# A block of attention and experts on one core: the first head group's rows written by their own products, and the first steps put in another order

## The reference

```python
# x: (4, 256, 128), ctx: (4, 64, 64); 16 heads of 8 columns
xn = layernorm(x)
q, k, v = xn @ Wq + bq, xn @ Wk + bk, xn @ Wv + bv            # per head
y  = softmax(causal(q k^T / sqrt(8))) v
qc, kc, vc = xn @ Wcq + bcq, ctx @ Wck + bck, ctx @ Wcv + bcv
y  = y + softmax(qc kc^T / sqrt(8)) vc
x  = x + y @ Wp + bp
h  = layernorm(x)
w  = weights of the 8 best of 32 experts by sigmoid(h @ Wr + br), normalized
x  = x + shared(h) + sum_e w_e * ((silu(h Wg_e + bg_e) * (h Wu_e + bu_e)) Wd_e + bd_e)
```

## Time and profile before

| | |
|---|---|
| median of 3 runs | 198.81 us (198.47 to 198.85) |
| the profiled execution | 198.38 us, its span 196.6 us |
| TensorE busy | 186.8 us (95%), 1254 matmuls |
| VectorE, ScalarE, GpSimd busy | 149.9, 137.6, 111.6 us |
| chain that ended last | PE 73%, POOL 14%, issue 5%, DVE 4% |

### The profile page before, as it was taken

The page is one execution under the profiler, slowest core; times in us unless marked ns, Lnnn a source line. Parts: engine busy times, 40 slices in busy tenths (PEclk is TensorE's granted clock), DMA queues, the critical chain, the costliest instruction groups (busy, mean ns, idle before and its releaser), DMA issues.

```text
span 196.6 us, 4006 instructions
## 1 busy us (share of the span) xinstructions
PE 186.8 (95%) x1254; PEld 138.8 (71%) x1254; DVE 149.9 (76%) x343; ACT 137.6 (70%) x280; POOL 111.6 (57%) x181
## 2 busy tenths in 40 slices
PE   7969999999999999998999999799999999999992
PEld 2537667777778777765775888588788888888671
DVE  2999997677659765896683879759777888887982
ACT  3546899787899887987788584875655556555471
POOL 6889994556396699839936567776622333000020
PEclk9999999999999999999999999999999999999999
DMA  4454423232243333500211103030000000000003
GB/s 114 107 144 122 122 71 79 57 80 68 63 105 95 77 80 76 132 12 17 66 42 43 40 0 80 12 77 17 0 0 0 3 0 0 0 2 0 3 0 107
DMA packets 20434, 10.40 MB, mean 53 GB/s; under 512 B 11881, under 2 KB 18542, under 8 KB 20414
## 3 DMA queue, kind: packets, MB, share of 16 engines
q1 hardware_dynamic: 19290, 9.24, 18.6%
q0 software_dynamic: 672, 0.69, 1.4%
q10 hardware_dynamic: 452, 0.23, 0.5%
HBM read 4.51 MB, written 0.52 MB: 26 GB/s over the span
## 4 chain that ended last, share of the span: by engine, by line
PE 73%; POOL 14%; issue 5%; DVE 4%; DMA 1%; ACT 1%; DVEq 0%; POOLq 0%
PE psum L1752 10%; PE psum L1417 7%; PE psum L1418 7%; PE psum L1419 7%; PE psum L1518 5%; PE psum L1574 5%; PE psum L1611 5%; PE psum L1599 5%; POOL hid_lo L739 4%; PE psum L1621 4%; PE psum L1517 3%; PE psum L1579 3%; POOL ckey_rows L457 3%; PE psum L1747 3%; PE psum L1583 2%
## 5 line engine op out<-in xcount | busy, mean ns | idle before, releaser
L982 ACT ACTIVATE gate<-psum,bias_cols 128x512 f32<-128x512 f32 (+2 forms) x35 | 23.5, 674 | 24.2 <-PE psum L1419 24.2
L844 ACT ACTIVATE probs<-psum 128x512 f32<-128x512 f32 x64 | 36.2, 596 | 2.3 <-PE psum L1579 1.1
L739 POOL TENSOR_TENSOR hid_lo<-hid,hid_hi 128x512 fp32r<-128x512 f32 x13 | 16.8, 1289 | 30.2 <-ACT hid_hi L991 30.1
L1361 DVE SCALAR_TENSOR_TENSOR gated<-psum,bias_cols,gate 128x512 f32<-128x512 f32 x32 | 24.0, 749 | 10.7 <-ACT gate L982 10.6
L1518 PE MATMUL psum<-key_blocks,query_rows 96*128 96x512 f32 x48 | 24.1, 544 | 0.0
L1373 DVE TENSOR_TENSOR hid<-gated,psum 128x512 f32<-128x512 f32 x32 | 21.9, 685 | 1.9 <-PE psum L1747 0.3
L658 POOL TENSOR_TENSOR w_late_lo<-w_ffn,w_late_hi 128x384 fp32r<-128x384 f32 x11 | 12.8, 1162 | 18.0 <-ACT w_late_hi L856 18.0
L991 ACT CAST hid_hi<-hid 128x512 fp32r<-128x512 f32 (+1 forms) x33 | 20.2, 613 | 2.5 <-DVE hid L1373 1.6
L1145 DVE TENSOR_REDUCE row_max<-psum 128x4 fp32r<-128x512 f32 x16 | 11.0, 688 | 13.4 <-PE psum L1518 13.3
L1149 DVE TENSOR_REDUCE row_max<-psum 128x4 fp32r<-128x1024 f32 x16 | 19.4, 1214 | 0.0
L1417 PE MATMUL psum<-xT_hi,w_late_hi 128*128 128x512 f32 x42 | 16.8, 400 | 0.1
(11 more groups left out here) (208 smaller groups left out, 516.6 us busy)
## 6 DMA issues: line engine op xcount, KB each, us to landing
query_rows<-queries SPq DMA_DIRECT2D x46, 64.0 KB, 2.1
key_rows<-keys SPq DMA_DIRECT2D x39, 32.0 KB, 1.9
w_ffn<-in_L_ffn_Wg SPq DMA_DIRECT2D x16, 64.0 KB, 1.9
w_ffn<-in_L_ffn_Wu SPq DMA_DIRECT2D x16, 64.0 KB, 2.1
w_ffn<-in_L_ffn_Wd SPq DMA_DIRECT2D x16, 64.0 KB, 2.0
ckey_rows<-ckeys POOLq DMA_DIRECT2D x12, 32.0 KB, 2.1
key_rows<-keys POOLq DMA_DIRECT2D x9, 32.0 KB, 2.2
x_sb<-in_x SPq DMA_DIRECT2D x2, 128.0 KB, 2.7
```

What stands on the lines that cost most here:

```text
L739: pool.tensor_tensor(hid_lo[:, n % 3, :], hid[:, n % 3, :], hid_hi[:, n % 3, :].bitcast(F32), ALU.subtract).then_inc(pool_lo_done, 1)
L844: act.activation(probs[:, i % 2, c, :], bank(B_ST + c % 2), ACT.Exp, scale=SCALE).then_inc(exp_done, 1)
L982: act.activation(gate[rows_of(n), n % 3, part], psum[of, B_GATE + n % 2, part], ACT.Silu, bias=bias_cols[of, BIAS_GATE + u:BIAS_GATE + u + ...
L1361: dve.scalar_tensor_tensor(out=gated[:, n % 3, :], in0=bank(B_UP + n % 2), scalar=bias_cols[:, BIAS_UP + u:BIAS_UP + u + 1], in1=gate[:, n ...
```

## The change

1. **Group 0 of batch 0 is not placed by DMA.** Its weights' 32 columns are written three times side by side (`w_direct_hi`, `w_direct_lo`, 96 columns), so `project_direct(k)` for keys, queries and cross queries gives the 96 rows at once. ScalarE rounds all 96 with the bias straight into `key_rows` and `query_rows` (`round_direct`), VectorE overwrites the 32 low rows (`split_direct`). The three parts of this group stand behind each other and not interleaved, so `head_mask` gets a second form. The biases get tripled columns too (`first_bias`).
2. **Batch 1 is not projected ahead of step 0.** `turn_x(1)` stands inside `natural(0)`, its norm goes from VectorE to ScalarE, and keys, queries and cross queries are projected between step 0's scores and `natural(1)`. Step 0's maxima are turned in two halves (`first_turn`, `first_shift`), so that its self scores start before its context maxima.
3. **Step 1 goes first.** VectorE takes step 1's maxima, and step 2's, before it splits batch 1's products; ScalarE expands step 1's and step 2's blocks, with all four heads for steps 2 and 3 (`ACT_ALONE`), around them.
4. **Values later.** Batch 1's values and the context values come in step 1 behind `natural(3)` (tail piece `values`). Value biases are no longer added to the values but once, as a column `y_bias`, when y has been turned.
5. **Context keys.** Batch 0's part of each group is expanded alone (`first_ctx`), the other three batches later (`later_ctx`, steps 0 to 3), all on GpSimd.
6. **Projections later.** `x_pair` goes from step 0 to the end of step 2, `keys_queries` and `cross_values` of batches 2 and 3 from steps 1 to 4 to steps 3 to 6. `x_pair` and `y_turn(0)` are the two turns that now stand behind the attention of their step.
7. **Two late edits.** At step 12 (`TURN_FIRST`, which is pass i = 12 of the loop) VectorE normalizes before it takes maxima. ScalarE's cast of `route_turn(2)` goes from item 6 slot B to item 5 slot C.
8. **Who issues.** SP places batch 0's keys of groups 1 to 3, the queries of groups 2 and 3, and the context keys of group 0; GpSimd the queries of group 1 and the other context keys; ScalarE issues no placement.

```diff
+ACT_ALONE = (2, 3)
+TURN_FIRST = 12
-        tail_at = {0: [("x_pair", FIRST_BATCHES)]}
-        for b in range(FIRST_BATCHES, BATCH):
-            tail_at[2 * b - 3] = [("keys_queries", b)]
-            tail_at[2 * b - 2] = [("cross_values", b)]
-        late_at = {}
+        tail_at = {1: [("values", 1)]}
+        for b in range(2, BATCH):
+            tail_at[2 * b - 1] = [("keys_queries", b)]
+            tail_at[2 * b] = [("cross_values", b)]
+        late_at = {2: [("x_pair", 2)], 6: [("y_turn", 0)]}
...
-                      (6, "B"): [("route_turn", 2)],
+                      (5, "C"): [("route_turn", 2)],
...
 # GpSimd, after rstd of tiles 2 and 3
+            place_ctx_keys(pool, 1)
+            pool.wait_ge(qkc_rounded, 3)
+            place_queries(pool, 0, 1, (0, 2))
+            place_ctx_keys(pool, 2, (0,))
+            first_ctx(0)
+            place_ctx_keys(pool, 2, (1, 2))
+            pool.wait_ge(qkc_split, 3)
+            place_queries(pool, 0, 1, (1,))
+            first_ctx(1)
+            place_ctx_keys(pool, 3)
...
 # ScalarE, ahead of the loop
+            round_direct(0)
+            round_direct(1)
+            round_qkc(0, 0)
+            expand(0)
+            round_qkc(0, 1)
+            round_qkc(0, 2)
+            round_direct(2)
...
+            norm(2)
+            norm(3)
+            round_x(1)
+            first_shift(0)
+            expand(1)
+            exps(0, (0,))
...
+            first_shift(1)
+            exps(0, (1,))
             expand(2)
+            round_qkc(1, 0)
+            shift(1)
             exps(0, (2, 3))
+            round_qkc(1, 1)
+            round_qkc(1, 2)
             for i in range(STEPS - 2):
...
+                if i == 2:
+                    act.wait_ge(have_neg_mean, 2)
+                    for t in range(4, TILES):
+                        norm(t)
...
 # VectorE
             maxima(0)
-            for n in range(3):
-                split_qkc(1, n)
...
-            expand(1)
-            expand_ctx(1)
-            expand(2)
             maxima(1)
-            cvalues()
             for i in range(STEPS):
...
                 if i + 2 < STEPS:
                     maxima(i + 2, i - 2)
+                if i == 0:
+                    for n in range(3):
+                        split_qkc(1, n)
...
+                if i == 1:
+                    expand(4)
+                    stats_of(2)
...
 # TensorE
+            project_direct(0)
+            project_direct(1)
+            pe.wait_ge(w_qkv_split, 1)
             project_qkc(0, 0)
             project_qkc(0, 1)
+            pe.wait_ge(pool_w_split, 1)
             project_qkc(0, 2)
-            project_values(0)
-            run_idle(7, B_NAT0)
-            turn_x(1)
...
+            pe.wait_ge(pool_w_split, 2)
+            project_direct(2)
+            run_idle(2, B_NAT1)
...
             natural(0)
-            project(1)
-            turn_max(0)
-            run_idle(3, B_MISC)
             for i in range(STEPS):
+                if i:
+                    scores(i, 0)
+                    scores(i, 1)
                 if i == 0:
-                    pe.wait_ge(qkc_split, 3 * FIRST_BATCHES)
-                scores(i, 0)
-                scores(i, 1)
-                if i == 0:
+                    pe.wait_ge(qkc_split, 3)
+                    project_values(0)
...
+                    project_qkc(1, 0)
+                    project_qkc(1, 1)
+                    pe.wait_ge(have_value, 1)
+                    project_qkc(1, 2)
                     natural(1)
-                    context_values()
-                    scores(0, 2)
                     scores(0, 3)
                 if i + 1 < STEPS:
                     turn_max(i + 1)
                 if i + 2 < STEPS:
                     natural(i + 2, i - 2)
+                    if i == 1:
+                        tail("values", 1)
```

More of the change, by code:

```diff
@@ L393, in value_bank @@
         def value_bank(b):
[L395 to L396 removed]
+            half = b > 0
+            return psum[:, B_MISC if half else B_OUT, SEQ * half:SEQ * (half + 1)]
         def turned_bank(i):
@@ new lines, in _ @@
+            act.wait_ge(t_bias, 1)
+            act.copy(bias_cols[:, BIAS_Q:BIAS_ROWS], bank(B_BIAS, 2 * BIAS_DIRECT)).then_inc(have_bias_cols, 1)
+            act.wait_ge(have_bias_cols, 1)
+            act.wait_ge(m_ck, 1)
+            act.activation(ckeys[:, 0, :], bank(B_CK, CTX_KEYS), ACT.Identity,
+                           bias=bias_cols[:, BIAS_CK:BIAS_CK + 1]).then_inc(ck_rounded, 1)
+            round_direct(0)
+            round_direct(1)
+            round_qkc(0, 0)
+            expand(0)
@@ L1018, in chain, with measure @@
                 dve.wait_ge(v_chain, chained[0])
-            def norm_stats(src, tiles, done):
+            def measure(src, tiles):
                 for k in range(tiles.start, tiles.stop):
@@ L1023, in norm_stats, with spread_of @@
                 chain(ins)
+            def spread_of(tiles, done):
                 for k in range(tiles.start, tiles.stop):
@@ L1027, in norm_stats @@
                 dve.tensor_scalar(var_eps[:, tiles], moments[:, tiles, 1], LN_EPS, None, ALU.add).then_inc(done, 1)
+            def norm_stats(src, tiles, done):
+                measure(src, tiles)
+                spread_of(tiles, done)
             def lo_half(dst, src, hi, done):
@@ L1171, in maxima @@
                 context()
-                if outputs >= 0:
+                if outputs >= 0 and not turn_first:
                     normalize(outputs)
@@ L1195, in tail @@
                     split_qkc(b, 1)
+                if name == "values":
+                    values(b)
+                    cvalues()
                 if name == "cross_values":
@@ L1625, in tail @@
             def tail(name, b):
-                reader = {"x_pair": xT_split, "keys_queries": qkc_split, "cross_values": have_value, "y_turn": yT_split, "project": x1_ready,
+                reader = {"values": have_value, "x_pair": xT_split, "keys_queries": qkc_split, "cross_values": have_value, "y_turn": yT_split, "project": x1_ready,
                           "x2_turn": x2T_split, "router": logits_ready,
@@ L1629, in tail @@
                 take_misc(reader, 3 * b + 2 if name == "keys_queries" else b + 1)
+                if name == "values":
+                    project_values(b)
+                    context_values()
                 if name == "x_pair":
@@ L1704, in _ @@
                 for name, b in tail_at.get(i, ()):
-                    tail(name, b)
+                    if name != "values":
+                        tail(name, b)
                 if i and i + 2 < STEPS:
```

518 lines of the change are left out of this document (299 added, 219 removed).

## The result

The changed kernel took 200.04 us (median of 21) against 198.85 for the kernel before (21 on the same chip), ratio 1.0064 (1.005 to 1.0079). On a second chip 199.97 against 198.46, ratio 1.0063 (1.0044 to 1.0082). The ratios leave out most of the long executions described next. The forecast was 198.1 and faster: wrong in sign, and outside its range. Of its three terms the two late edits held (route_turn 0.9, TURN_FIRST 0); the prologue's did not.

A forecast was written before the change was run, and what follows sets the result against it. GpSimd's DMA issues were taken to bound the kernel up to 25 us, TensorE's queue from 32.3. Terms +0.2, 0.0 and -0.9 gave -0.7 us, so 198.1 us by the median; 8 in 10 range 196.3 to 199.8.

The forecast's parts named there:

- route_turn 0.9: Expert stage: ScalarE's cast moved to item 5 lets TensorE go on 0.9 us earlier (bounds 0 and 0.95).
- TURN_FIRST 0: Step 12: normalizing before maxima on VectorE gains 0 (bounds 0.1 us later to 0.5 earlier).
- the prologue's: Prologue and steps 0 to 6: step 7 starts 0.2 us later than before (bounds 2.0 earlier to 1.6 later).
- `natural(0)` at 10.1: Prologue: ScalarE ends `expand(0)` at 10.0, so `natural(0)` starts at 10.1 against 14.58, 4.5 us earlier.
- `scores(0, 0)` 13.7, `natural(1)` 16.7, `natural(2)` 20.5: Prologue and first rounds: forecast start times in us of these three TensorE products; `scores(0, 0)` was at 19.31 before.
- The landing that was argued over at length: Before `natural(1)`: group 1's last query rows, issued at 14.05, land after 2.6 us, so it starts at 16.7.
- The 0.5 us of slack: Before `natural(1)`: `expand(1)` beside GpSimd has 0.5 us to spare; 0.3 added for it and `expand(4)` together.
- `natural(3)` at 24.65: Round of step 3: ScalarE alone expands four blocks at 0.45 each, ready at 24.6, holding `natural(3)` until 24.65.
- Step 2, 5.5 us: Step 2, from 30.5: given 4.77 plus 0.35 of `x_pair`, and 0.35 lost as `scores(3, 0)` waits for ScalarE.
- Steps 3 to 5: Moved projections: step 3 has keys and queries 2 plus 0.3 for ScalarE; steps 4 and 5 take 5.74 and 5.48.
- Rival A: `natural(1)` to `attend_self(0)`: rounds cost more than the lead, step 7 is 1.5 us later, time 199.4; chance 0.25.
- The clock: Prologue, where fillers are fewer: a granted clock under 1.00 would show the forecast wrong; no size or chance given.

The follow-up runs named there:

- after_turn6: Changed kernel with `y_turn(0)` back in step 6's tail instead of behind its attention; 201.14 us, ratio 1.0147 to the kernel before.
- fill_share3: `after_fill` with step 3's blocks shared again between VectorE and ScalarE and no fillers before `natural(3)`; 198.69 us, ratio 1.0001 to the kernel before.
- fill_stats: `after_fill` with `stats_of(2)` ahead of `expand(4)` on VectorE at the end of step 1; ratio 1.0022 to the kernel before.
- fill_late: Changed kernel with three filler products more, in the wait before `natural(3)`; 199.38 and 199.45 us, ratios 1.0045 and 1.0055 to the kernel before.
- fill_noturn: `after_fill` with step 12 in the old order, maxima ahead of normalizing on VectorE; ratio 1.004 to the kernel before.
- before_route: Kernel before with only ScalarE's `route_turn(2)` cast moved from item 6 to item 5; 197.57 us, ratio 0.9952.
- after_fill: Changed kernel with seven filler products more in TensorE's waits, up to the one before `natural(3)`; 199.29 us, ratio 1.0036 to the kernel before.

## Why the prediction was wrong, step by step

- **`natural(0)` at 10.1: measured 10.65.** The prediction took ScalarE's end of `expand(0)` as the last and gave the hop a tenth. ScalarE ends at 10.16, but VectorE, with two splits of 0.48 and two blocks of 0.62, at 10.29, and TensorE starts 0.36 later. That hop could be read in the rows: VectorE's blocks end at 13.57 + 0.62 = 14.19, `natural(0)` starts at 14.58, 0.39 us. Direct product 0 started 0.2 late as well.
- **`scores(0, 0)` 13.7, `natural(1)` 16.7, `natural(2)` 20.5: 14.17, 17.25, 21.09.** The same half microsecond carried on. The landing that was argued over at length was not the last: VectorE's `expand(1)` ended at 17.14, in 2.16 us, and with the blocks at 0.87 `natural(1)` started at 16.90 (`after_turn6`). The 0.5 us of slack that it was credited with was eaten. (GpSimd's queue adds up to 14.15, not 14.05, and the last low part was issued at 14.44.)
- **`natural(3)` at 24.65, for ScalarE's four blocks: 25.53.** Right cause, 0.9 late; the half microsecond, and a hop of 0.25 behind the blocks. It was named and not weighed: two of them fit VectorE's idle time, worth 0.5 us at the start of step 2 (`fill_share3`), of which step 3 keeps only what `expand(4)` leaves.
- **Step 2, 5.5 us: 6.36.** This is the failed step, the largest single miss of the sum. The prediction charged it to ScalarE's norms (0.35). VectorE set it: `negative_mean(2)` stands ahead of `maxima(4)` in its queue and waits for GpSimd's rstd, whose input is computed behind `expand(4)`. The prediction knew that `expand(4)` feeds the rstd, and put 0.3 on everything of that kind; it did not write out VectorE's queue for step 2. `fill_stats` and `fill_late` show both parts, the order (0.47) and the stretching (0.42): without them step 2 takes 5.47, the 5.5 forecast.
- **Steps 3 to 5: as planned**, 5.47, 5.75, 5.48, and without the extra 0.3 for ScalarE. **Step 6: 6.17 for 5.97**, 0.15 of it a wait for VectorE's copy out of the shared bank. Step 7 came at 60.40, 1.2 behind the 59.2 forecast and 1.4 behind the kernel before. Rival A had 1.5 there, in part by luck: the two stretchings came true, the late landing didn't, and more than half of the loss fell in step 2, behind `attend_self(0)`, where A's place ends. A had 0.25 because the forecast leaned on the old rounds having been stretched as well.
- **TURN_FIRST at 0: right** (`fill_noturn`). **route_turn -0.9: right** (`before_route`).
- **Behind step 7, some 0.8 us of span that no term held:** 0.2 in step 8 (the late place of `y_turn(0)`, by `after_turn6`), 0.3 in step 12, 0.1 before `x2_turn(3)` and 0.2 in the late items. It takes back nearly all of the 0.9 of the route_turn edit. Another 0.2 is around the span (its median runs from 1.71 to 1.98 from kernel to kernel, and within `after_fill` from 1.69 to 2.02; cause open). The prediction counted the stretch as unchanged because its work is.
- **The clock** stood in the list of what would make it wrong, with no chance or price. The price was 2.3 to 3.8 us in 8 of 31 executions, but since the medians and the ratio leave most of it out, it isn't what turned the sign.

The forecast's method, level points and what was given work, was sound; its largest fault is that VectorE's queue wasn't written out to the end, while VectorE set three of the four late landmarks (`natural(0)`, `natural(1)` and `attend_self(1)` in step 2).

## What to carry to other kernels

Write out the queue of every engine between two level points, and for each wait in it what is queued behind: a small operation that waits (0.47 us of `negative_mean`) in front of a large one on the path costs the whole wait. Add the hop that the trace shows between the last producer's end and the first product, here 0.36, at every round of a latency-bound stretch. When a prologue is thinned, price the clock by what follows the idle time, and put filler products in each new wait; they cost nothing that the profiles here show, and saved 2.3 to 3.8 us in a quarter of the executions.

## What the runs showed of the hardware that was not expected

- A fall of the granted clock to the 1.2 GHz level came here with no long wait ahead of it: 0.33 and 0.84 us of idle time within two microseconds, in some executions of one program and not in others.
- VectorE's two blocks took 0.62 us alone and 1.04 against one GpSimd select of 0.63. Beside a GpSimd expansion of 0.63 and three DMA issues of together 1.51 they took 2.16 when they started 0.03 us behind the expansion, and 0.87 when they started 0.18 behind it. The 2.16 is more than the expansion can hold the port for by the rule above; whether the DMA issues hold VectorE too was not isolated.
- A gap of 0.22 us on VectorE comes and goes with two instructions more in its program, and costs 0.3 us where the engine is on the path. That it is the reading of instructions was only argued.
- The same expert items took 2.27 or 2.29 us by where their buffers lie: 192 bytes moved them from one to the other.
